# Attention stage of a fused transformer layer: normalised rows written four tiles ahead in two buffers and turned by transposing transfers instead of on TensorE

## The reference

```
h = einsum(x, weighted_sum, weight); h = concat([h, txt])          # 589 x 8 tokens, 256 wide
n = layernorm(h)                                                   # (h - mean) / sqrt(var + eps)
q, k, v = split(n @ in_proj_weight.T + in_proj_bias)               # 16 heads of 16
attn = softmax(l2norm(q) . l2norm(k) * exp(min(logit_scale, ...))) # over the 8 sequences' positions
h = h + ((attn @ v) * head_scale) @ out_w.T + out_b
h = h + ffn(layernorm(h))                                          # second attention, 8 gated experts
```

## Time and profile before

| what | value |
|---|---|
| median of 3 runs | 804.05 us (800.21 to 805.13) |
| the profiled execution | 801.38 us, of which the span from the first to the last instruction is 799.3 us |
| mean granted TensorE clock | 0.981 of full speed |
| TensorE busy | 745.6 us (93%) |
| VectorE busy | 703.5 us (88%) |
| ScalarE busy | 374.4 us (47%) |
| GpSimd busy | 409.4 us (51%) |

### The profile page before, as it was taken

The page is one execution under the profiler, slowest core; times in us unless marked ns, Lnnn a source line. Parts: engine busy times, 40 slices in busy tenths (PEclk is TensorE's granted clock), DMA queues, the critical chain, the costliest instruction groups (busy, mean ns, idle before and its releaser), DMA issues.

```text
span 799.3 us, 48197 instructions
## 1 busy us (share of the span) xinstructions
PE 745.6 (93%) x20274; PEld 508.0 (64%) x20274; DVE 703.5 (88%) x1591; ACT 374.4 (47%) x985; POOL 409.4 (51%) x1094
## 2 busy tenths in 40 slices
PE   4999978999999999876999999999999999999997
PEld 3888855666666666654656666666666666666553
DVE  5798778999999999765799999999999999999987
ACT  4478544665566665543333443344344434343321
POOL 1231355555666667444455665566556655665411
PEclk9999999999999999987899999999999999999999
DMA  9987000000000000000011001100111011101100
GB/s 331 326 252 228 3 3 4 2 0 0 0 0 0 0 0 2 11 17 10 15 26 28 23 16 26 26 23 16 26 26 26 14 26 26 26 13 27 29 16 20
DMA packets 38377, 33.25 MB, mean 42 GB/s; under 512 B 24786, under 2 KB 33570, under 8 KB 38314
## 3 DMA queue, kind: packets, MB, share of 16 engines
q1 hardware_dynamic: 38314, 32.35, 13.4%
HBM read 22.64 MB, written 4.83 MB: 34 GB/s over the span
## 4 chain that ended last, share of the span: by engine, by line
PE 39%; DVE 10%; issue 3%; DVEq 0%
PE bank L204 9%; PE bank L205 8%; PE bank L206 8%; PE bank L957 5%; PE bank L946 5%; DVE acc L1099 3%; DVE smax L1108 2%; PE bank L964 1%; DVE res L1099 1%; PE bank L977 1%; PE bank L1016 1%; PE bank L1003 1%; PE bank L1002 1%; DVE fq_t L1147 1%; DVE logits L1117 1%
## 5 line engine op out<-in xcount | busy, mean ns | idle before, releaser
L1099 DVE SCALAR_TENSOR_TENSOR acc<-bank,gate,acc 128x256 f32<-128x256 f32 x222 | 106.1, 478 | 12.8 <-PE bank L206 4.1
L204 PE MATMUL bank<-we_h,h_t_h 128*128 128x512 f16 x296 | 113.0, 382 | 3.7 <-DVE res L1099 1.0
L205 PE MATMUL bank<-we_l,h_t_h 128*128 128x512 f16 x296 | 112.2, 379 | 0.6 <-issue 0.6
L206 PE MATMUL bank<-we_h,h_t_l 128*128 128x512 f16 x296 | 112.2, 379 | 0.0
L204 PE MATMUL bank<-tokw_h,x_t_h 128*128 128x256 f16 x256 | 71.0, 277 | 11.3 <-DVE x_t_l L682 11.3
L1053 ACT ACTIVATE junk<-x 128x256 f32<-128x256 f32 x37 | 15.4, 417 | 120.4 <-DVE x L1143 120.4
L205 PE MATMUL bank<-tokw_l,x_t_h 128*128 128x256 f16 x256 | 70.9, 277 | 0.0
L206 PE MATMUL bank<-tokw_h,x_t_l 128*128 128x256 f16 x256 | 70.8, 277 | 0.0
L1188 POOL TENSOR_TENSOR t<-ss,rms_ws 128x1 f32<-128x1 f32 x37 | 7.1, 192 | 117.1 <-ACT junk L1053 117.1
L287 PE MATMUL bank<-vaug,pr_t 32*32 32x17 f32 x4736 | 49.8, 181 | 10.7 <-issue 10.7
L957 PEld LDWEIGHTS bank<-pr_t,v 32*32 32x32 f32 x4736 | 47.6, 104 | 18.7 <-issue 18.3
(11 more groups left out here) (223 smaller groups left out, 2232.8 us busy)
## 6 DMA issues: line engine op xcount, KB each, us to landing
xbuf<-in_x SPq DMA_DIRECT2D x32, 512.0 KB, 5.3
out<-res SPq DMA_DIRECT2D x36, 128.0 KB
we_s<-in_we SPq DMA_DIRECT2D x4, 512.0 KB, 7.3
inw<-in_in_w SPq DMA_DIRECT2D x1, 768.0 KB, 11.6
hn_t_h<-hn_r_h SPq DMA_TRANSPOSE x37, 2.3
hn_t_l<-hn_r_l SPq DMA_TRANSPOSE x37, 2.4
wrep<-in_w_rep SPq DMA_DIRECT2D x1, 512.0 KB, 4.8
h_all<-in_txt SPq DMA_DIRECT2D x1, 512.0 KB
```

The lines of the kernel that those rows point to most:

```text
L204: nc.tensor.matmul(dst, a_h(c), b_h(c), start=start and c == 0, stop=False)
L205: nc.tensor.matmul(dst, a_h(c), b_l(c), start=False, stop=False)
L206: last = nc.tensor.matmul(dst, a_l(c), b_h(c), start=False, stop=stop and c == chunks - 1)
L1099: op = nc.vector.scalar_tensor_tensor(out=(res if e == E - 1 else acc)[:, :], in0=b_we[s % 2][:, k * D:(k + 1) * D], scalar=gate[p][:, e:e ...
```

## The change

The rows xn get two buffers, and beside them the high and the low half xn_r, also twice. ScalarE writes high half and full rows of tile i+4 in body i, behind the exponential; GpSimd subtracts them for the low half in front of its root steps; SP issues two transposing transfers per tile, from SBUF to SBUF, which fill xt. A transfer for tile j waits for the rows (a_xn), for the v product of tile j-2, which is the last reader of that xt (a_vm), and for the transfers of the tile before (xn_in). TensorE waits on xn_in. The transposition on TensorE and both splits behind it go, and with them one PSUM bank's use. On ScalarE the moments of tile i-3 move behind the copy of v. The entries in the image stage begin one body earlier (-4). The diff, shortened:

```diff
-        xn = sb("xn", [P, D])
+        xn = [sb(f"xn{p}", [P, D]) for p in range(2)]
+        xn_r = [halves(f"xn_r{p}", [P, D]) for p in range(2)]
@@ attn_pe, body
                 if real(i, 2):
-                    pe.wait_ge(a_xtl, i + 3)
+                    pe.wait_ge(xn_in, 32 * (i + 3))
...
                 if real(i, 1):
-                    pe.wait_ge(a_xtl, i + 2)
+                    pe.wait_ge(xn_in, 32 * (i + 2))
...
-                if real(i, 3):
-                    pe.wait_ge(a_xn, i + 4)
-                    wait(pe, a_xtl, i + 3)
-                    for c in range(KC):
-                        last = nc.tensor.transpose(b_xt[:, c * P:(c + 1) * P], xn[:, c * P:(c + 1) * P], ident[:, :])
-                    last.then_inc(a_xnps, 1)
@@ attn_act
+            def rows(i, p):
+                if real(i, 4):
+                    settle(act, tokw_ready)
+                    wait(act, p_xnl, i + 3)
+                    wait(act, xn_in, 32 * (i + 3))
+                    at = bass.ds(i + 4, 1)
+                    for to in (xn_r[p][0], xn[p]):
+                        last = nc.scalar.activation(to[:, :], h_all[:, at, :].squeeze(1), ACT.Identity,
+                                                    bias=cf_all[:, at, NM:NM + 1].squeeze(1),
+                                                    scale=cf_all[:, at, RS:RS + 1].squeeze(1))
+                    last.then_inc(a_xn, 1)
...
                 if real(i, 0):
                     act.wait_ge(a_sub, i + 1)
                     wait(act, a_prt, i)
                     nc.scalar.activation(pr[:, :, :], sc[:, :, :], ACT.Exp).then_inc(a_exp, 1)
+                if part != 1:
+                    rows(i, p)
+...
-                if real(i, 3):
-                    act.wait_ge(a_xnps, i + 4)
-                    wait(act, a_vm, i + 2)
-                    nc.scalar.activation(xt[1 - p][0][:, :, :], b_xt[:, 0:D], ACT.Copy).then_inc(a_xth, 1)
@@ attn_dve, end of body
-                if real(i, 3):
-                    dve.wait_ge(a_xth, i + 4)
-                    nc.vector.tensor_tensor(xt[1 - p][1][:, :, :], b_xt[:, 0:D], xt[1 - p][0][:, :, :],
-                                            ALU.subtract).then_inc(a_xtl, 1)
@@ attn_pool, start of body
+                if real(i, 4):
+                    pool.wait_ge(a_xn, i + 5)
+                    nc.gpsimd.tensor_tensor(xn_r[p][1][:, :], xn[p][:, :], xn_r[p][0][:, :], ALU.subtract).then_inc(p_xnl, 1)
@@ new
+        def attn_turn(sp, j):
+            sp.wait_ge(a_xn, j + 1)
+            wait(sp, a_vm, j - 1)
+            wait(sp, xn_in, 32 * j)
+            sp.dma_start_transpose(xt[j % 2][0][:, :, :], xn_r[j % 2][0][:, :]).then_inc(xn_in, 16)
+            sp.wait_ge(p_xnl, j + 1)
+            sp.dma_start_transpose(xt[j % 2][1][:, :, :], xn_r[j % 2][1][:, :]).then_inc(xn_in, 16)
@@ first block, sync, at the end
+                for j in range(2):
+                    attn_turn(sp, j)
@@ first block, scalar
                     if i == ENTRY:
                         act.wait_ge(nm_ready, 2)
+                        attn(-4, 0, 0)
+                    if i == ENTRY + 1:
                         attn(-3, 1, 0)
-                    if i == ENTRY + 3:
-                        attn(-3, 1, 1)
+                    if i == ENTRY + 5:
                         attn(-2, 0, 0)
@@ first block, gpsimd, at the end
+                attn_pool(pool)(-4, 0)
+                attn_pool(pool)(-3, 1)
                 attn_pool(pool)(-2, 0)
@@ second block, sync, ahead of the feed-forward stage's loop
+                for j in range(2, TILES):
+                    attn_turn(sp, j)
```

More of the change, by code:

```diff
@@ L262, in build @@
         WU_AT, TXT_AT, BIAS_AT, LS_AT, BVEC_AT, ENTRY = 19, 5, 13, 20, 22, 25
-        names = ("ls_ready", "a_xn", "a_xnps", "a_xth", "a_xtl", "a_qkm", "a_vm", "a_sq", "a_qkr", "a_v", "a_ss", "a_half",
+        names = ("ls_ready", "a_xn", "p_xnl", "xn_in", "a_qkm", "a_vm", "a_sq", "a_qkr", "a_v", "a_ss", "a_half",
                  "a_shift", "a_guess", "a_qk", "a_qkt", "a_s", "a_max", "a_sub", "a_exp", "a_prt", "a_av", "a_rsum",
@@ L267, in build @@
                  "bvec_ps", "bvec_ready")
-        (ls_ready, a_xn, a_xnps, a_xth, a_xtl, a_qkm, a_vm, a_sq, a_qkr, a_v, a_ss, a_half,
+        (ls_ready, a_xn, p_xnl, xn_in, a_qkm, a_vm, a_sq, a_qkr, a_v, a_ss, a_half,
          a_shift, a_guess, a_qk, a_qkt, a_s, a_max, a_sub, a_exp, a_prt, a_av, a_rsum,
@@ L271, in build @@
          bvec_ps, bvec_ready) = map(sem, names)
-        b_xt, b_qk, b_v, b_s, b_o, b_ot = bank[0], (bank[1], bank[7]), *bank[2:6]
+        b_qk, b_v, b_s, b_o, b_ot = (bank[1], bank[7]), *bank[2:6]
         b_out = b_ot[:, D:2 * D]
@@ L358, in turned @@
                     nc.scalar.activation(on_h[:, :, :], b_ot[:, 0:D], ACT.Copy).then_inc(a_onh, 1)
+            def rows(i, p):
[9 more added lines that the diff above has]
+                    last.then_inc(a_xn, 1)
             def body(i, p, part=None):
+                if part == 0:
+                    return rows(i, p)
                 if part == 3:
                     return turned(i)
[L363 to L371, removed]
                 if real(i, 0):
@@ L375, in body @@
                     nc.scalar.activation(pr[:, :, :], sc[:, :, :], ACT.Exp).then_inc(a_exp, 1)
+                if part != 1:
+                    rows(i, p)
+                if real(i, 2):
+                    act.wait_ge(a_qkm, i + 3)
+                    wait(act, a_ss, i + 2)
+                    nc.scalar.activation(sq[:, :, :], b_qk[p][:, :], ACT.Square, scale=1.0 / WS).then_inc(a_sq, 1)
+                    wait(act, p_kpad, i + 1)
+                    nc.scalar.activation(kr[p][:, :], b_qk[p][:, D:2 * D], ACT.Copy, scale=ROOT * ROOT / WS).then_inc(a_qkr, 1)
+                if real(i, 1):
+                    act.wait_ge(a_vm, i + 2)
+                    wait(act, a_av, i)
+                    nc.scalar.activation(vaug[1 - p][:, :, 0:HD], b_v[:, 0:D], ACT.Copy, scale=1.0 / WS).then_inc(a_v, 1)
                 if real(i, -3):
```

## The result

The changed kernel took 818.72 us (median of 4 runs, 815.50 to 824.26) against 804.59 us of the kernel before (4 runs, 800.21 to 806.25): ratio 1.0202 with an interval of 1.0160 to 1.0244. Predicted were 805.7 us and a range of 799 to 814. So the change makes the kernel some 2% slower, and the forecast missed that. The profiled execution took 815.50 us.

What follows compares the result with a forecast made beforehand. The steady loop was taken as bound by a round trip through VectorE and TensorE, 6.37 us per tile. Terms -0.44 + 2.5 - 0.44 + 0 = +1.6 us on the median 804.05 gave 805.7 us, range 799 to 814.

Steps and rivals of the forecast that it cites:

- xt_l is worth 0 in the loop: Attention loop, VectorE: deleting the 0.42 us low-half subtraction only leaves idle time before smax; period stays 6.37 us.
- The transpositions are worth 0 in the loop: Attention loop, TensorE: removing the 0.22 us slot only lengthens the wait for k_t from 0.28 to 0.50 us.
- The covers on ScalarE and GpSimd: Attention loop: idle time on both engines hides the added row writes (at most 0.60 us) and 0.67 us subtraction; cost 0.
- The transfers' loop ties at 6.35: Attention loop: transfer round trip 3.80 plus TensorE's 2.55 makes 6.35 us against 6.37 per tile; cost 0 over 28 periods.
- Port collision: Attention loop: GpSimd's subtraction and VectorE block each other, at most +7.6 us if every tile; chance 0.03, of which 0.02 slower.
- VectorE as bound: Attention loop: VectorE is the bound after all, period 5.97, -11 us, but -0.6 with the transfers deciding; chance 0.05.
- The image stage: Attention tiles 0 and 1, among the image tiles: TensorE is the bound, so removing two transposition slots gives -0.44 us.
- The start of the stage: First attention bodies: late transfers nearly hidden, but two TensorE clock falls, in bodies 0 and 1, cost +2.5 us (bounds 0 and 3.8).
- The maximum 3.9 of the earlier trace: Attention loop: longest landing from issue, in us; if it came every tile, the loop would be 7.85 and cost +41 us.
- the transfers land late: Attention loop: late landings make TensorE wait, +8 to +41 us; chance 0.13 of over 1%, 0.14 of a smaller loss.
- The end and the later stage: About two tiles ending the attention stage: TensorE is the bound, so removing the transpositions gives -0.44 us.
- a chance of 0.01 for losses that couldn't be priced: Hand-over from attention to the next stage: possible slowdown of unstated size, chance 0.01.

Runs made afterwards that it cites:

- moments_first: The changed kernel with ScalarE's two moments back directly behind the exponential; 821.58 us, ratio 1.0217 to the kernel before.
- start_buffers: The changed kernel with separate buffers for the transposed rows of tiles 2 to 4; 810.57 us, ratio 1.0094 to the kernel before.
- v_first: The changed kernel with the v product ahead of the q and k product on TensorE; 808.33 us, ratio 1.0084 to the kernel before.
- plain_copies: The changed kernel with ordinary transfers instead of transposing ones, so the turning is left out; 811.89 us in one run.
- v_first_padded: v_first plus two unread identity transpositions per body on TensorE, restoring the old code length; 806.14 us, ratio 1.0057 to the kernel before.
- shifted kernels: The kernel before with 100 or 28 tiny matmuls added at the start of TensorE's program; 809.48 us (1.0089) and 808.54 us (1.0071).
- padded kernels: v_first with two idle transpositions per body: alone, with VectorE reordered, and with ScalarE's moments also last; ratios 1.0057, 1.0010 and 0.9953.

## Why the prediction was wrong, step by step

- **xt_l is worth 0 in the loop: right.** Predicted period 6.37, idle 0.4 before smax, released by the scores; measured 6.37, 0.31, the scores.
- **The transpositions are worth 0 in the loop: right.** The wait for k_t was to become 0.50 and became 0.43.
- **The covers on ScalarE and GpSimd: right.** GpSimd has 1.02 idle before the root (predicted: about 1), ScalarE 2.26 before the exponential (about 1.5, too careful).
- **The transfers' loop ties at 6.35: right for the loop.** The 22 transfers between 160 and 300 us landed after 2.3 to 2.4, and the product waited for only the first of them, 0.15 us. No run tells how narrow the tie was: what slows the loop of moments_first is the squares, not the transfers.
- **Port collision, VectorE as bound: neither came.** The subtraction takes 0.67 as in the earlier trace rows.
- **The image stage: the sign was right, the size can't be told.** A0 came 1.04 earlier, -0.44 was predicted. But in four more kernels with the same removal (start_buffers, v_first, moments_first, plain_copies) it came between 0.90 earlier and 0.09 later.
- **The start of the stage, "two clock falls = +2.5 (bounds 0 and 3.8)": this is the step that failed.** From A0 to A7 it cost 1.04 + 7.95 = 9.0. The prediction put 3.80 from the end of v to the start of the product, with the later stage's median landing in it. By SP's issue times, which follow v by 0.04, the three took 109.00 - 104.47 = 4.53, 117.86 - 113.17 = 4.69 and 126.66 - 120.43 = 6.23. That is 4.05 more than 3 x 3.80, and the third, which had been given no wait at all, waited 3.14. The number of clock falls was right, two, but the second came in body 2 rather than in body 1, behind that wait. The delays were also not hidden: the wait for k_t of the earlier trace rows covered the first only in part, since the late product ran on the lower clock, and the third held ss and then smax of tile 3. start_buffers and v_first both take the loss at A3 away (+0.09 and +0.66 instead of +6.52): shown.
- **The maximum 3.9 of the earlier trace rows was read as a price "every tile", with +41 us.** It was neither spread over the tiles nor rare by chance. Late landings sit in the straight code, just where the stage has no slack. The rival "the transfers land late" had the right mechanism and the wrong place; its price where it holds is 4.05 us of waits and what they cost behind.
- **The end and the later stage, the second "-0.44" and a chance of 0.01 for losses that couldn't be priced: failed.** From A7 to F36 the changed kernel lost 5.75 more, 2.77 of it between F5 and F6. The sum has no term for what taking instructions out does to the code behind. v_first shows the loss apart from the start, v_first_padded takes it away at that place, and the shifted kernels produce such losses without the change.

For the profiled execution the account is: image tiles -1.04, start +8.99, loop -0.03, A31 to F5 +0.90, F5 to F6 +2.77, F6 to F36 +2.11, sum +13.70. The start's part is settled by experiment, the part at F5 to F6 as well. That the +0.90 is position is argued from the shifted kernels (+1.69 and +1.34 there) and from the stalls between 300 and 460 us, 13.4 us against 10.3. The +2.11 is less sure. It comes with one wait for code of 1.51 us at 780.64, and the kernel with 100 tiny matmuls has the same one (1.24), but the two shifted kernels lose hardly anything from F6 to F36 (-0.01 and +0.19).

Three things stay open. Why a transfer is late when an instruction block crosses it is not shown beyond the coincidence. Why a block comes late at one place and in time at another is not known, and the padded kernels show that it isn't the place alone. And v_first_padded stays at 1.0057 in the median while its profiled execution, the shortest of seven, is level with the kernel before. Own buffers at the start together with v first, and other code lengths, were not tried.

## What to carry to other kernels

Read a latency where it will be waited for: a median over 37 transfers is that of the loop, and the first tiles of a stage, in straight code, pay the maximum, with a lower clock behind some of the waits. When a transfer takes an in-order step's place, order the last reader of its buffer first and its next reader last; here that one swap gave back more than half of the loss. And before a difference of 1% is put down to an idea, look whether it sits in code that the idea doesn't touch, and run a version padded to the old length.

## What the runs showed of the hardware

- A 64 KB transposing transfer inside SBUF landed 2.3 to 2.4 us after its issue in the loop and took 1.17 to 1.25 us of SP's queue; a plain one landed after 1.9 to 2.0. With an instruction block under way they took up to 4.5 and 3.7.
- The position of TensorE's code moved the time by 0.7 to 0.9% (28 or 100 added tiny matmuls, +5.9 and +7.7 us). It acts through stalls of TensorE of up to 2.6 us, nearly all among small matmuls of the straight code, each ending 1.19 to 1.60 us after an instruction block has landed (151 of 151 in 13 traces).
- The Trainium skill (Runtime: NRT & Kernel Launch, "Instruction fetch mechanics") has instructions fetched in blocks of 16 KiB, as the 0.02 MB of each block here agrees with. It has the fetch hidden behind the issue. The traces agree for most blocks and not for all: 10 stalls for 33 blocks between 100 and 460 us of the kernel before.
- The clock fell behind idle times of 3.25 and 3.14 us after small matmuls (granted 0.54 and 0.61 over the next 4 us), but also behind 2.12 (changed kernel, 136.12), 1.31 and 0.76 (start_buffers, 143.93); it stayed up behind 2.00, 1.40 (v_first) and 0.91 (the kernel before, 142.93). The length of the idle time alone doesn't decide it.
